# 64-expert layer: two of eight row fetches and two of five unread products in the ranking's block, the others in the next block

## The reference, cut to what matters

```python
logits = xf @ gate_w + gate_b
top_l, top_i = jax.lax.top_k(logits, K)            # K = 3
gates = jax.nn.softmax(top_l, axis=-1)
fe = top_i.reshape(-1)
oh = jax.nn.one_hot(fe, E, dtype=jnp.int32)        # E = 64
pos = (jnp.cumsum(oh, axis=0) * oh).sum(-1) - 1
valid = pos < C                                    # C = 64
buf = jnp.zeros((E, C, D), x.dtype).at[fe, pos].set(xf[tok], mode='drop')
h = jax.nn.gelu(jnp.einsum('ecd,edh->ech', buf, w1) + b1[:, None, :], approximate=False)
y = jnp.einsum('ech,ehd->ecd', h, w2) + b2[:, None, :]
rows = y[fe, jnp.minimum(pos, C - 1)] * (fg * valid.astype(x.dtype))[:, None]
out = jnp.zeros_like(xf).at[tok].add(rows)
```

## Time and profile before

| what | us |
|---|---|
| median of three runs | 1845.82 (1844.06 to 1846.3) |
| the profiled execution, its own time | 1841.34 |
| its span | 1839.5 |
| the ranking's block | from 364.8 to 403.6 |
| the expert block | from 403.6 to 512.3 |
| PE busy over the span | 1565.9 |
| POOL busy over the span | 432.8 |

### The profile page before, as it was taken

The page is one execution under the profiler, slowest core; times in us unless marked ns, Lnnn a source line. Parts: engine busy times, 40 slices in busy tenths (PEclk is TensorE's granted clock), DMA queues, the critical chain, the costliest instruction groups (busy, mean ns, idle before and its releaser), DMA issues. The chain is left out here.

```text
span 1839.5 us, 21220 instructions
## 1 busy us (share of the span) xinstructions
PE 1565.9 (85%) x7428; PEld 694.9 (38%) x7428; DVE 847.9 (46%) x1637; ACT 762.3 (41%) x1379; POOL 432.8 (24%) x386
## 2 busy tenths in 40 slices
PE   6857778639946999999999999977999998776997
PEld 2223332325523333333333333324565564123443
DVE  5842278443333555455545545524343334524343
ACT  3443345334434656565655655541222224342111
POOL 1000062026401455455545445420000000100000
PEclk9978889759956999999999999997999999887999
DMA  8200030529240000000000000020000000000000
GB/s 279 92 12 0 26 81 1 191 80 345 100 122 1 1 1 1 1 1 1 1 1 1 1 0 1 1 98 1 1 0 0 0 0 29 1 30 27 0 0 23
DMA packets 32494, 71.27 MB, mean 39 GB/s; under 512 B 5747, under 2 KB 19827, under 8 KB 31375
## 3 DMA queue, kind: packets, MB, share of 16 engines
q1 hardware_dynamic: 30358, 65.93, 10.4%
q0 software_dynamic: 2048, 4.20, 0.8%
HBM read 65.92 MB, written 7.34 MB: 40 GB/s over the span
## 5 line engine op out<-in xcount | busy, mean ns | idle before, releaser
L1762 DVE TENSOR_REDUCE a_nmp<-a_SP 128x2 bf16<-128x590 f32 (+1 forms) x256 | 197.0, 769 | 267.5 <-PE a_SP L1531 265.6
L1690 ACT ACTIVATE a_prob<-a_TP 128x512 f32<-128x512 f32 x256 | 138.9, 595 | 154.8 <-PE a_TP L1519 153.7
L1549 PE MATMUL a_O<-a_prob,a_V 128*64 128x512 f32 (+1 forms) x640 | 172.2, 617 | 1.5 <-DVE a_on L1800 1.5
L1516 PE MATMUL a_TP<-a_qn,a_kn 64*128 64x512 f32 (+1 forms) x640 | 166.3, 597 | 1.0 <-DVE a_negm L1825 0.5
L1847 POOL TENSOR_TENSOR a_acc<-a_acc,a_prob 128x512 f32<-128x512 f32 x128 | 158.7, 1271 | 2.3 <-DVE a_acc L1813 1.6
L1245 DVE TENSOR_TENSOR f_hv<-f_gl,f_VP 128x512 f32<-128x512 f32 (+1 forms) x96 | 65.8, 686 | 163.5 <-ACT f_gl L1211 163.5
L1211 ACT ACTIVATE f_gl<-f_HP 128x512 f32<-128x512 f32 (+1 forms) x96 | 57.2, 595 | 200.7 <-PE f_VP L1193 200.7
L1837 POOL TENSOR_TENSOR a_acc<-a_prob 128x512 f32<-128x512 f32 x64 | 79.8, 1266 | 205.1 <-ACT a_prob L1690 205.1
L818 POOL TENSOR_TENSOR a_kxb<-a_kT,hmu 128x1232 bf16<-128x1232 f32 x9 | 21.7, 2409 | 414.4 <-DVE a_kxb L606 367.7
L1180 PEld LDWEIGHTS f_YP<-f_W,f_hv 128*128 128x128 f32 (+1 forms) x768 | 100.5, 192 | 47.9 <-issue 44.3
L1191 PE MATMUL f_HP<-xn,f_W 128*128 (+1 forms) x192 | 104.1, 625 | 16.4 <-PEq L1095 11.0
(11 more groups left out here) (377 smaller groups left out, 2776.6 us busy)
## 6 DMA issues: line engine op xcount, KB each, us to landing
ring_w<-in_F_w SPq DMA_DIRECT2D x64, 512.0 KB, 8.3
f_yg<-dispatched SPq DMA_DIRECT2D x12, 256.0 KB, 5.3
a_maskT<-in_maskT SPq DMA_DIRECT2D x4, 576.0 KB
a_biasT<-in_biasT SPq DMA_DIRECT2D x1, 2304.0 KB
f_b<-in_F_b SPq DMA_DIRECT2D x1, 1664.0 KB, 8.5
f_W<-in_F_w SPq DMA_DIRECT2D x1, 1536.0 KB, 11.9
f_W<-in_F_w SPq DMA_DIRECT2D x1, 1408.0 KB, 6.2
f_V<-in_F_v SPq DMA_DIRECT2D x1, 1408.0 KB, 9.1
```

Of the source, the lines that this page charges most:

```text
L1516: nc.tensor.matmul(TP[0:hi - lo, h, :], kn[HALF[h], g % 4, lo:hi], qn[HALF[h], g % 4, :], start=True, stop=False)
L1549: mm = nc.tensor.matmul(O[HALF[h], :], V[0:n, g % 4, kc, HALF[h]], prob[0:n, kc, h, :], start=kc == 0, stop=kc == NC - 1)
L1690: nc.scalar.activation(prob[0:n, kc, h, :], TP[0:n, h, :], ACT.Exp, bias=rowneg[0:n, g // NP:g // NP + 1] if kc == 0 else 0.0)\
L1762: nc.vector.tensor_reduce(nmp[:, u // 2, u % 2, :], SP[:, :, 0:hi - lo], AX.X, ALU.max, negate=True).then_inc(s_used, 1)
```

## The change

The constant FIRST = 2 is new. In the ranking's block POOL issues `fetch(0)` and `fetch(1)` only; `fetch(2)` to `fetch(7)` become the first instructions of POOL in the expert block, ahead of its wait for `rows_zeroed`. Two of the five unread products move too: PE makes them at the end of its list in the ranking's block, into XP, after a wait for the last of ACT's four copies out of XP; three stay ahead of `turn(0)`.

```diff
-    XR, BR, YR, BEHIND, WARM = 8, 4, 4, 4, 5
+    XR, BR, YR, BEHIND, FIRST, WARM = 8, 4, 4, 4, 2, 5
...
                         mm.then_inc(indexed, 1)
+                    pe.wait_ge(tok_ready, G)
+                    for i in range(2):
+                        nc.tensor.matmul(XP[:, i, :], c.center[:, :], c.xn[:, 0:S], start=True, stop=True)
...
                     pool.wait_ge(slot_in_made, 1)
-                    for n in range(XR):
+                    for n in range(FIRST):
                         fetch(n)
...
+                for n in range(FIRST, XR):
+                    fetch(n)
                 pool.wait_ge(c.rows_zeroed, 2 * 16)
                 for n in range(PAIRS):
...
-                for _ in range(WARM):
+                for _ in range(WARM - 2):
                     nc.tensor.matmul(HP[:, 1, :], c.center[:, :], c.xn[:, 0:512], start=True, stop=True)
                 turn(0)
                 turn(1)
```

## The result

The changed kernel took 1833.48 us as the median of four runs (1829.49 to 1835.68), against 1846.03 for the kernel before (four runs): ratio 0.9932 with a 95% interval of 0.9913 to 0.9951. Twice more it was timed beside the kernel before, at 0.9965 (0.9955 to 0.9974) and 0.9952 (0.9938 to 0.9965). So it is faster each time, by 6.5 to 12.5 us; the forecast was 8.85.

A forecast was written before the change was run, and what follows sets the result against it. PE sets the loop's pace, but POOL's fetches alone hold the border before the expert block; -7.50 (fetches) and -1.35 (products), with 0 for `turn(2)`, sum to -8.85 us, from median 1845.82 to 1837.0, range 1833 to 1842.

The forecast's parts named there:

- The border: Ranking's block to expert block: POOL alone holds it, so moving six fetches behind it gains 7.50 us, bounds -7.5 and 0.
- the 3.15 that I let stay: Time from POOL's last fetch in the ranking's block to the next block's start, 3.15 us, forecast to stay.
- 2.7 + 0.47 = 3.17: At the border: an unloaded fetch's landing plus a DVE-ended border, close to 3.15; POOL may end only when fetches have landed.
- Two products ahead of the border: End of PE's list in the ranking's block: 3.4 us at the low clock, hidden behind POOL, warming nothing that survives.
- rival B: Expert block's start: clock already high from the moved products, part of the gain lost to `turn(2)`'s wait; sum -9.8, chance 0.11.
- Three products behind it: Expert block's start: six records instead of ten before the first transpose, -1.35 us, bounds -2.3 and -0.8.
- C: Expert block's start: clock does not rise during the three products, only 8 us behind the border; sum -7.2, chance 0.09.
- D: Expert block's first pairs: clock stays low for long; 20 us of it gives 1846.9, eight pairs 1860; chance 0.04.
- The term of 0 to +0.4: `turn(2)` in the expert block: wait for fetch 2 flying beside b2, put at 0, bounds 0 and +0.4 us.
- the prediction's own sign of being wrong: Expert block: the prediction would be wrong if, among other signs, `turn(2)` waited for more than a microsecond.
- rival A: Expert block: fetch 2 queues behind all of b2, `turn(2)` waits 2.1 us; sum -6.8, 1839.1, chance 0.10.
- Nothing is paid here: POOL in the expert block: later fetches and first scatter delay nobody, and POOL keeps up in the loop; no cost.

The follow-up runs named there:

- FIRST = 0: Changed kernel with no fetch in the ranking's block, all eight behind the border, and b2's loads held until the third transpose; ratio 0.993 to the kernel before.
- the slowed fetches: Changed kernel plus an unneeded 2 MB DRAM-to-DRAM copy by SP, flying beside fetches 0 and 1; 1839.05 us in its one execution.
- the first trace: Profiled execution of the changed kernel itself, from its first measurement against the kernel before; timed there at 1833.48 us, ratio 0.9932.
- the third trace: Profiled execution of the unchanged changed kernel, run again in the third round beside the kernel before; ratio there 0.9952.
- the fourteen traces: All traces of this case, kernel before and variants; last scatter to next block 7.36 to 7.37 us with 56 POOL transfers, 8.01 with 64.
- the first round: Against the kernel before: changed kernel again 0.9965, fetches alone 0.9962, products alone 0.9999, changed kernel without the two products in the ranking's block 0.9974.
- the run meant to test them: Changed kernel with SP issuing a pair's weights only when those of the pair before have landed; ratio 0.998 to the kernel before.

## Why the prediction was right

**The border: right.** -7.50 was forecast and -7.69 measured from the first fetch on (12.11 to 4.42). The 0.2 over it are the 3.15 that I let stay: behind two fetches they were 2.9 to 2.95 in the three traces of the changed kernel. POOL alone held the border, as FIRST = 0 showed, and the reading that its landings do was an inference from 2.7 + 0.47 = 3.17; the slowed fetches showed it.

**Two products ahead of the border: right that they are free; that they warm nothing held in two traces of three.** In the first trace they took 2.76 and not 3.4, since the clock rose under them at 389.0. By the Trainium skill ("TensorE: Matmul & The Clock Gate", section "What's actually happening") idling brings the low clock back; the trace agrees, with 0.50 again from 392.5, 2.3 us after the products' end at 390.22. In the third trace it was still 1.00 for 0.9 us behind the border, after 3.10 us of idling: rival B in small, and as that rival has it the wait of `turn(2)` took part of the gain back. Of the six traces with FIRST = 2, both products and an undelayed border this is the only one, so it is the rarer course and not an excluded one. The version with FIRST = 0 idled for 0.79 and kept 1.00.

**Three products behind it: right in the trace, not seen in the times.** 5.07 to the first transpose (4.6 to 5.2 was forecast), 1.32 less than before (1.35); 4.34 in the third trace. Rivals C and D did not come: the clock rose 4.8 behind the border, at 399.2, and held. But the products alone gave a ratio of 0.9999, and the fetches alone as much as the whole change, so no timed run shows a gain of this part.

**`turn(2)`: the size was off.** The term of 0 to +0.4 was worth 0.8 of waiting, 1.4 and 1.1 in two other traces; more than a microsecond was the prediction's own sign of being wrong, and two traces of three show it. I took 6 us for a fetch beside b2 and let the loop's slowest, 6.5, stand as the bound; it was 7.1 (402.1 - 395.02). The Trainium skill ("DMA: Bandwidth & Descriptors", section "Queues, rings and completion order") has the engines take turns between queues, by which the term would have been 0; the measured landing lies between that and rival A's wait for all of b2 (8.9 behind the border; it was 7.7). In the end it cost 0.3 to 0.8 of the loop, since first intervals of 2.61, 2.91 and 3.15 stand against 2.34.

**The end of the block: put at nothing, and it costs 0.5.** "Nothing is paid here" looked at when POOL's transfers start and not at the block's end. From the last scatter's start to the next block it was 502.50 - 494.64 = 7.86, before 512.30 - 504.93 = 7.37, and the table of the fourteen traces shows that this is no chance but 0.08 for each of the six moved fetches. It isn't the last landing either: the last scatter landed 2.2 to 2.3 after its start in the six traces that show it, some 5 us ahead of that border. What POOL does in those microseconds is open. The expert block's -0.55 is -1.32 + 0.27 + 0.49.

**The sum.** -8.85 was forecast for code that gave -8.22 in one profiled pair of executions; the 0.6 between them are what the forecast put at nothing, -0.2 at the border, +0.3 at `turn(2)` and +0.5 at the block's end. The timed gains of 12.5, 6.5 and 8.8 scatter around it, and in the traces the causes of that lie outside the change: ramps of the clock in other stages, and the late starts of the first round. So the 1833.48 of the result is partly luck: it lies 3.5 below the 1837.0 of the forecast and 0.5 inside its range, and 3.6 us of the profiled pair's difference came from stages with the same code. The cause of the late starts stays open; they came under the ring's loads and in one round only, and the run meant to test them met none.

## What to carry to other kernels

A block border waits for what POOL has in flight, so look for the last *landing* of POOL, not for its last issue, and move transfers that the next block needs late to its far side. Here it paid to move all of them, though PE then waited 0.8 us twice for the first ones. It is not so for every queue: SP's loads flew over a border for 7 us and more. A transfer moved away isn't free of the border: it adds 0.08 us at the next one. Nor does it fly alone: it meets what other queues issue at the same moment, and holding back the large load that nobody needs yet took the wait away, though the total didn't show it. And products meant to warm the clock pay only if little idle time follows: 0.8 us kept what they raised, and 3.0 to 4.2 us lost it ahead of the border in all traces but one.

## What the runs showed that I had not expected

The border waited for landings even when these took 6.6 and 7.9 us. A fetch of 64 KB beside 2 MB of other loads lands after 6.6 to 7.9 us, alone after 2.4 to 3.1. The border at the end of the expert block stands 5 us behind POOL's last landing and grows by 0.08 us for each transfer of POOL's in the block, 56 to 64 of them. And the same program can lose 7 to 10 us in a loop of 88 in which DVE and ACT start late though PE's product is there, in four executions of four in one round and in none of eight in the other two.
